# Each row gather waits for TensorE's side sum sixteen steps back instead of ten steps back

## The chip, the cores and the metric

The kernel runs on one core of one Trainium2 chip. The metric is the device time of one execution in microseconds (us), as the median of several runs. Engines are named as in the profile: PE is TensorE (PEld its weight loads), DVE is VectorE, ACT is ScalarE, POOL is GpSimd, SP is SyncE, whose queue starts the plain transfers.

## The reference

Four graph layers are applied one after the other to 12,500 nodes of 128 features and 200,000 edges sorted by target; each is added to its input and normalised. The parts that matter here are the edge parts: for each edge the row of its source node is fetched, a score is formed from it and the target's row, the scores are turned into weights by a softmax over the edges of one target, and the weighted rows are summed into the target. The first layer (two attention layers in it) reads:

```
xl = x @ Wl + bl
xr = x @ Wr + br
xj = xl[src]
e = jax.nn.leaky_relu(xj + xr[dst], NEG_SLOPE)
logits = e @ att
m = jax.ops.segment_max(logits, dst, num_segments=n)
ex = jnp.exp(logits - m[dst])
denom = jax.ops.segment_sum(ex, dst, num_segments=n)
alpha = ex / (denom[dst] + EPS)
out = jax.ops.segment_sum(alpha[:, None] * xj, dst, num_segments=n)
```

## The kernel before

Edges are laid out in tiles of 128, one tile being one **step**; 16 steps (`G`) make a **turn**, and a layer has 104 turns. Four edge stages share one set of functions, with an object `Edges` for each: E0 and E1 (gathering from `gather_a` and `gather_b`, one head), E2 (`gather_s`, scores from node scores alone, so that `vector` is false), and E3 (`gather_c`, eight heads). Between E1 and E2 lies another stage, S1, that scatters by source, and before, between and after them lie dense stages over the nodes.

In an edge stage every engine runs its own stream of instructions, and semaphores alone tie them together; nothing is reordered. In the turn with number `it`:

- SP (`sp_edges`, L658) loads the turn's tables into one of four slots: edge columns with the source indices (L665), one-hot rows, row values (L666, L667), step rows (L669; eight of them in E3). It waits until the sums of the turn four back have been added.
- POOL (`pool_edges`, L676) issues 16 gathers a turn (L687), one for each step: 128 rows of 512 bytes into `rows`, in slot `it % 4`. It waits for the tables of the turn (L682), for the block sums of the turn four back, which read the slot last (L684), and, before each gather, for a side sum (L686). This last wait is the subject. It guards no data: the slot is free by L684.
- PE (`side`, L708) goes through the turn in four chunks of four steps. For a chunk it waits until its four gathers have landed (L711), and then makes for each step a **side sum**: the target's row by a one-hot matrix (L721) plus the gathered row by the identity (L722). In E2 the side sum (L725) reads no gathered row. Behind each chunk's side sums PE makes one-hot distances for a later chunk (L705, L747), the **block sums** of the turn two back (L738), and a small transpose (L774, L779, L782 or L789, one for each chunk).
- ACT makes one-hot matrices (L811, L826) and the sloped scores (L862). DVE makes scores (L908, L915, L921), scans for the softmax, and adds block sums into the targets' sums (L951; L960 in E3).

A side sum of step `g` counts one up on the semaphore `side_sums`; `L.side.at(it, g)` is the count after step `g` of turn `it`, and `lag=1` takes the same step of the turn before. `hold_ge` is a wait. `Fori` loops run over four turns with the counts in registers; the first eight turns are written out.

Of the kernel before, what the change touches and what calls it, by code (L numbers as in the profile page):

```python
# [16 lines left out]
G = 16  # L17
# [1 line left out]
PEEL = 2 * U  # L19
CH = 4  # L20
NCH = G // CH
LEAD = 10
AW = 136
XW = 130
NSUM = 4
# [135 lines left out]
def turns(eng, n, depth, turn, ahead=0):  # L161


    assert ahead <= U
    end = n - U if ahead else n
    for i in range(PEEL):
        turn(Turn(i))
    with eng.Fori(PEEL // U, end // U) as j:
        for u in range(U):
            turn(Turn(u, j))  # L170
    for i in range(end, n + depth):
        turn(Turn(i))


def build(nc, a, out):
# [31 lines left out]
    with ExitStack() as ctx:  # L207
# [468 lines left out]
        def pool_edges(e, L):  # L676
            w = On(e, anchor)
            w.wait_ge(L.opened.at(0))

            def turn(it):  # L680
                u = it.slot()
                w.hold_ge(L.tab.at(it))  # L682
                for c in range(NCH):
                    w.hold_ge(L.block.at(it, c, lag=U))  # L684
                    for g in range(c * CH, (c + 1) * CH):
                        w.hold_ge(L.side.at(it, g - LEAD) if g >= LEAD else L.side.at(it, g + G - LEAD, lag=1))  # L686
                        e.indirect_dma_start(rows[:, u, g, 0:L.width], None, L.src_rows,  # L687
                                             bass.IndirectOffsetOnAxis(ap=edge_sb[:, u, g:g + 1].bitcast(I32), axis=0)
                                             ).then_inc(L.gat[c].sem(it), 16)
            turns(e, NG, 0, turn)  # L690
# [1786 lines left out]
```

## Time and profile before

| What | Value |
|---|---|
| median of 3 runs | 14976.3 us (14975.89 to 14977.52) |
| the profiled execution's own time | 14998.3 us |
| its span, first to last instruction | 14996.4 us |
| PE, DVE, ACT, POOL busy | 74%, 53%, 37%, 63% of the span |
| gathers in each edge stage | 1664 (104 turns of 16) |

Busy shares are averages over stages that are limited by different things, so they say little by themselves. "Idle before" in a row is how long the engine stood still just before an instruction, and the name behind the arrow is what the profile believes ended it: "issue" means that the profile sees no wait that ended there, and "remote" that a semaphore moved and the profile does not know by whom.

### The profile page before, as it was taken

To read this page: it belongs to the slowest core of one execution; us is meant where nothing else is said; L and a number is where in the kernel's file an instruction comes from. 1 tells how busy PE (TensorE), PEld (TensorE's weight loads), DVE (VectorE), ACT (ScalarE), POOL (GpSimd) and SP (SyncE) were. 2 spreads that over 40 slices of the span, in tenths; PEclk is the share of its full clock that TensorE was granted. 3 is DMA by queue.
4 is the path that set the end of the run, shared out by engine and by line. 5 is a ranking of instruction groups with operands and counts; after the bars stand their busy time and mean duration, and the time that the engine had idled before them with its cause. 6 is when DMAs were issued, how large, how long until landed. Compare 5 with 4: busy or idle time off the path is not lost.

```text
span 14996.4 us, 278163 instructions
## 1 busy us (share of the span) xinstructions
PE 11026.0 (74%) x60653; PEld 8678.6 (58%) x60653; DVE 7973.5 (53%) x29240; ACT 5541.4 (37%) x14105; POOL 9489.8 (63%) x8593
## 2 busy tenths in 40 slices
PE   5777777777777778888888875555555767777776
PEld 4666666666666666666666653344344556666664
DVE  6555555555555555555555553333333566666666
ACT  1444444344444444333333343333333622222223
POOL 3666666466666657888888865566666255655555
PEclk7887788788778775766666765555555877888777
DMA  3111111221111113444444452222222221222222
GB/s 87 45 45 44 44 45 45 88 80 44 45 44 45 44 40 44 39 39 39 39 39 39 39 104 58 44 45 45 45 45 45 60 52 48 50 49 49 50 50 56
DMA packets 808955, 748.01 MB, mean 50 GB/s; under 512 B 264685, under 2 KB 691174, under 8 KB 808254
## 3 DMA queue, kind: packets, MB, share of 16 engines
q0 software_dynamic: 453440, 550.05, 21.1%
q1 hardware_dynamic: 354814, 191.38, 4.9%
q14 instruction: 599, 4.91, 0.1%
q8 instruction: 102, 1.67, 0.0%
HBM read 548.62 MB, written 192.13 MB: 49 GB/s over the span
## 4 chain that ended last, share of the span: by engine, by line
PE 27%; another core or an unknown queue 15%; issue 13%; DMA 9%; DVE 7%; ACT 6%; POOL 2%; SPq 1%; DVEq 1%; ACTq 0%; POOLq 0%
DMA scatter_s<-dst_side 8%; PE bank L738 8%; PE bank L721 3%; PE bank L722 3%; PE bank L1214 3%; ACT oh_e L826 2%; PE bank L1220 2%; PE bank L1229 2%; PE bank L747 2%; PE bank L705 1%; POOL scatter_s L1181 1%; DVE agg L960 1%; DVE lrelu L915 1%; DVE agg L951 1%
## 5 line engine op out<-in xcount | busy, mean ns | idle before, releaser
L738 PE MATMUL bank<-rows,oh_e 128*128 128x130 f32 x9984 | 2172.6, 376 | 1578.7 <-ACT oh_e L826 1172.1
L1181 POOL DMA_INDIRECT scatter_s<-dst_side x1664 | 2568.6, 1544 | 551.9 <-DMA scatter_s<-dst_side 267.1
L738 PEld LDWEIGHTS bank<-rows,oh_e 128*128 128x128 f32 x9984 | 1804.0, 264 | 1918.7 <-issue 1036.4
L826 ACT ACTIVATE oh_e<-bank,weight,minus_w 128x128 f32<-128x128 f32 x4992 | 1880.3, 459 | 2378.4 <-remote 1620.8
L951 DVE SCALAR_TENSOR_TENSOR agg<-agg,rescale,bank 128x130 f32 x4992 | 1683.4, 337 | 1636.6 <-remote 792.6
L722 PE MATMUL bank<-rows,ident 128*128 128x128 f32 x9984 | 2335.9, 319 | 144.8 <-issue 141.1
L687 POOL DMA_INDIRECT rows<-gather_c,edge_sb x1664 | 1650.9, 992 | 1122.4 <-issue 443.9
L687 POOL DMA_INDIRECT rows<-gather_b,edge_sb x1664 | 1672.5, 1005 | 1061.9 <-issue 423.0
L687 POOL DMA_INDIRECT rows<-gather_a,edge_sb x1664 | 1669.1, 1003 | 1008.5 <-issue 412.0
L687 POOL DMA_INDIRECT rows<-gather_s,edge_sb x1664 | 1574.3, 946 | 1061.2 <-issue 443.2
L722 PEld LDWEIGHTS bank<-rows,ident 128*128 128x128 f32 x9984 | 1894.7, 235 | 159.7 <-issue 157.6
L862 ACT ACTIVATE lrelu<-bank 128x512 f32<-128x512 f32 x1248 | 751.2, 602 | 2734.9 <-PE bank L722 1900.8
L721 PE MATMUL bank<-dst_side,oh_t 128*128 x4992 | 1253.8, 338 | 202.5 <-issue 116.5
L721 PE MATMUL bank<-dst_side,hT 128*128 x4992 | 1232.0, 334 | 96.9 <-issue 93.2
L908 DVE TENSOR_TENSOR lrelu<-lrelu,bank 128x512 f32<-128x512 f32 x1248 | 850.5, 681 | 714.4 <-ACT lrelu L862 520.0
L705 PE MATMUL bank<-oh_rows,oh_w 5*128 5x512 bf16 x1664 | 788.6, 474 | 556.5 <-ACT oh_t L811 290.5
L721 PEld LDWEIGHTS bank<-dst_side,oh_t 128*128 128x128 f32 x4992 | 950.9, 236 | 311.4 <-issue 280.7
L721 PEld LDWEIGHTS bank<-dst_side,hT 128*128 128x128 f32 x4992 | 932.2, 232 | 194.5 <-issue 153.8
L1214 PE MATMUL bank<-rows,dst_side 128*128 128x130 f32 x3328 | 775.0, 399 | 343.1 <-DVE dst_side L1290 325.8
L1299 DVE SCALAR_TENSOR_TENSOR dst_side<-iota,edge_sb,bank 128x98 f32<-128x98 f32 x1664 | 432.4, 315 | 1115.9 <-PE bank L1220 1078.3
L738 PE MATMUL bank<-xw,oh_e 128*128 128x136 f32 x3328 | 620.4, 339 | 510.5 <-DVE xw L931 218.2
L1214 PEld LDWEIGHTS bank<-rows,dst_side 128*128 128x128 f32 x3328 | 653.2, 278 | 577.0 <-DVE dst_side L1290 359.6
(352 smaller groups left out, 18169.2 us busy)
## 6 DMA issues: line engine op xcount, KB each, us to landing
rows<-gather_a,edge_sb POOLq DMA_INDIRECT x1664
rows<-gather_b,edge_sb POOLq DMA_INDIRECT x1664
scatter_s<-dst_side POOLq DMA_INDIRECT x1664
rows<-gather_s,edge_sb POOLq DMA_INDIRECT x1664
rows<-gather_c,edge_sb POOLq DMA_INDIRECT x1664
rows<-scatter_s SPq DMA_DIRECT2D x56, 455.0 KB, 6.3
scatter_s<-zeros SPq DMA_DIRECT2D x64, 390.0 KB
edge_sb<-edge_tab SPq DMA_DIRECT2D x520, 40.0 KB
```

The lines of the kernel that those rows point to most:

```text
L687: e.indirect_dma_start(rows[:, u, g, 0:L.width], None, L.src_rows, bass.IndirectOffsetOnAxis(ap=edge_sb[:, u, g:g + 1].bitcast(I32), axis= ...
L705: e.matmul(bank[0][:, :], oh_w[:, :], oh_rows[:, it.slot(lag), c * CH * P:(c + 1) * CH * P], start=True, stop=True).then_inc(L.dist.sem, 1)
L721: e.matmul(o, oh, dst_flat[:, bass.ds(at[g], P)], start=True, stop=False)
L722: e.matmul(o, ident[:, :], rows[:, it.slot(), g, 0:P], start=False, stop=True).then_inc(L.side.sem, 1)
L738: ins = e.matmul(sum_bank(g)[:, (g % 2) * AW:(g % 2) * AW + L.aw], oh_e[:, g % 8, :], r, start=True, stop=True)
L826: e.activation(oh_e[:, g % 8, :], bank[7][:, (g % CH) * P:(g % CH + 1) * P], ACT.Relu, bias=weight[:, it.slot(2, 2), g:g + 1], scale=minus ...
L862: e.mul(lrelu[:, c % 2, :], bank[2 + c % 2][:, :], SLOPE).then_inc(L.sloped.sem, 1)
L908: e.tensor_tensor(lrelu[:, c % 2, :], lrelu[:, c % 2, :], bank[2 + c % 2][:, :], ALU.max).then_inc(L.larger.sem, 1)
L951: e.scalar_tensor_tensor(old, old, rescale[:, it.slot(2, 2), g:g + 1], sum_bank(g)[:, (g % 2) * AW:(g % 2) * AW + L.aw], ALU.mult, ALU.add ...
L1181: e.indirect_dma_start(scatter_s[k], bass.IndirectOffsetOnAxis(ap=S_.target[:, it.slot(1), g:g + 1], axis=0), S_.summed[:, g % 8, :], None ...
L1214: e.matmul(bank[6 + h % 2][:, (g % 2) * XW:(g % 2 + 1) * XW], S_.same[:, g % 8, :], rows[:, v, g, :], start=True, stop=True).then_inc(S_.b ...
L1299: e.scalar_tensor_tensor(S_.scratch[:, g % CH, 0:NB], iota[:, 0:NB], edge_sb[:, u, 4 * G + g:4 * G + g + 1], bank[5][:, (g % CH) * P:(g % ...
```

## The change

The constant `LEAD` goes, and with it the choice in L686. Before, the gather of step g waited for the side sum ten steps earlier: of the same turn where g is 10 or more, else of the turn before. Now it waits for the side sum of the same place in the turn before, sixteen steps earlier. Everything else stays, the waits for tables and block sums included. Line numbers below the removed constant fall by one.

```
-LEAD = 10
...
                 for c in range(NCH):
                     w.hold_ge(L.block.at(it, c, lag=U))
                     for g in range(c * CH, (c + 1) * CH):
-                        w.hold_ge(L.side.at(it, g - LEAD) if g >= LEAD else L.side.at(it, g + G - LEAD, lag=1))
+                        w.hold_ge(L.side.at(it, g, lag=1))
                         e.indirect_dma_start(rows[:, u, g, 0:L.width], None, L.src_rows,
```

No instruction of any engine changes its place. What differs on POOL is the count that a wait compares with, and that the first turn of a stage has no such wait at all. The start of E0 on POOL before, from the last index loads of the preparation (`tcoli`, L409) to the second turn:

```order
L409 DMA rows<-in_src_dram,tcoli 128x128 [waits edge_columns_made] x11
L687 DMA rows<-gather_a,edge_sb 128x128 [waits tables_in_slot0,rows_and_carry_set]
L687 DMA rows<-gather_a,edge_sb 128x128 x9
L687 DMA rows<-gather_a,edge_sb 128x128 [waits side_sums] x6
L687 DMA rows<-gather_a,edge_sb 128x128 [waits side_sums,tables_in_slot1]
```

And the same place now:

```order
L408 DMA rows<-in_src_dram,tcoli 128x128 [waits edge_columns_made] x11
L686 DMA rows<-gather_a,edge_sb 128x128 [waits tables_in_slot0,rows_and_carry_set]
L686 DMA rows<-gather_a,edge_sb 128x128 x15
L686 DMA rows<-gather_a,edge_sb 128x128 [waits side_sums,tables_in_slot1]
L686 DMA rows<-gather_a,edge_sb 128x128 [waits side_sums] x15
```

The six gathers of the first turn that waited for a side sum wait no more; from the second turn on each gather has its wait as before, on a lower count.

## Rows read from the trace of the kernel before

**Rows 1.** Busy time by stretch: E0, E1, then E2, E3.

```profile
core 0: us, PE busy (x) PEld busy (x) DVE busy (x) ACT busy (x) POOL busy (x), PEclk, DMA share, GB/s
220.00:2850.00 2630.00, 2031.69 (x12444) 1660.33 (x12444) 1433.82 (x4292) 1083.40 (x2760) 1668.83 (x1664) 0.81 0.18 45
2950.00:5585.00 2635.00, 2048.70 (x12444) 1668.62 (x12444) 1434.82 (x4295) 1087.42 (x2760) 1672.49 (x1664) 0.80 0.20 55
...
9090.00:11700.00 2610.00, 1408.97 (x7464) 1021.18 (x7464) 844.75 (x3365) 868.93 (x2345) 1574.27 (x1664) 0.50 0.21 46
12025.00:14780.00 2755.00, 2058.97 (x12627) 1700.82 (x12628) 1827.85 (x5108) 786.22 (x1949) 1650.52 (x1664) 0.81 0.20 50
```

**Rows 2.** What POOL's gathers waited for, E0's loop: releaser, us, times.

```profile
L687 POOL DMA_INDIRECT rows<-gather_a,edge_sb x1609: 941/947/1763, 301.4 to 2849.4; - x179
  PE bank L722: 311.6, 218
  remote: 201.7, 102
```

**Rows 3.** What PE waited for, E0's loop (us, times, longest).

```profile
PE bank L738 <- ACT oh_e L826: 237.1, 100, 5.7
PE bank L721 <- issue: 76.4, 102, 1.8
```

**Rows 4.** POOL in order of time, E0: start, us, gather, [idle before].

```profile
449.86 0.94 POOL L687 DMA_INDIRECT rows<-gather_a,edge_sb  x1 [1.86 <-PE bank L722]
451.11 1.67 POOL L687 DMA_INDIRECT rows<-gather_a,edge_sb  x1 [0.30 <-issue]
...
455.58 1.47 POOL L687 DMA_INDIRECT rows<-gather_a,edge_sb  x1 [0.30 <-issue]
```

**Rows 5.** PE's order of time: first and last late chunk of E0, E1, E3.

```profile
458.83 0.48 PE L721 MATMUL bank<-dst_side,hT 128*128 x2 [0.71 <-issue]
2847.47 0.48 PE L721 MATMUL bank<-dst_side,hT 128*128 x2 [1.08 <-issue]
3158.97 0.79 PE L721 MATMUL bank<-dst_side,oh_t 128*128 x2 [0.21 <-issue]
5582.06 0.48 PE L721 MATMUL bank<-dst_side,hT 128*128 x2 [0.90 <-issue]
12079.29 0.48 PE L721 MATMUL bank<-dst_side,oh_t 128*128 x2 [1.81 <-DMA rows<-gather_c,edge_sb]
14658.72 0.79 PE L721 MATMUL bank<-dst_side,oh_t 128*128 x2 [2.27 <-DMA rows<-gather_c,edge_sb]
```

**Rows 6.** SP's, POOL's and PE's order of time around one late chunk of E3.

```profile
13349.22 3.73 SPq L669 DMA_DIRECT2D step_sb<-step_tab  x8
13355.38 1.39 POOL L687 DMA_INDIRECT rows<-gather_c,edge_sb  x1 [3.05 <-issue]
13362.78 0.48 PE L721 MATMUL bank<-dst_side,oh_t 128*128 x2 [2.32 <-DMA rows<-gather_c,edge_sb]
```

**Rows 7.** PE and SP in order of time over two turns of E0.

```profile
1500.28 0.42 PE L774 MATMUL bank<-ident,masked 128*16 128x128 f32 x1
1520.33 0.29 PE L774 MATMUL bank<-ident,masked 128*16 128x128 f32 x1
1523.18 0.01 SPq L669 DMA_DIRECT2D step_sb<-step_tab  x1
1546.88 0.27 PE L774 MATMUL bank<-ident,masked 128*16 128x128 f32 x1
```

**Rows 8.** The chain that ended last, within E1: shares by line.

```profile
by line: another core or an unknown queue 21.0%; issue 15.4%; PE bank L738 15.1%; PE bank L721 12.6%; PE bank L722 11.9%; ACT oh_e L826 3.1%; PE bank L747 2.7%; PE bank L705 2.7%; DVE agg L951 2.7%; DVE lrelu L915 1.4%; DVE lrelu L908 1.2%;
```

**Rows 9.** DVE's longest wait in E2's loop, and who waited for gathers there.

```profile
DVE rescale L978 <- remote: 836.6, 81, 12.0
  DMA rows<-gather_s,edge_sb: 7.9, 1
```

**Rows 10.** DVE's groups in E0's loop: line, count, busy us, mean ns.

```profile
L915 DVE TENSOR_TENSOR lrelu<-lrelu,att 128x512 f32<-128x512 f32 x404 | 270.3, 669 | 0.8
```

More of the change, by code:

```diff
@@ L21 @@
 NCH = G // CH
-LEAD = 10
 AW = 136
@@ L685, in turn @@
                     for g in range(c * CH, (c + 1) * CH):
-                        w.hold_ge(L.side.at(it, g - LEAD) if g >= LEAD else L.side.at(it, g + G - LEAD, lag=1))
+                        w.hold_ge(L.side.at(it, g, lag=1))
                         e.indirect_dma_start(rows[:, u, g, 0:L.width], None, L.src_rows,
```

## The prediction

> **What bounds the kernel now.** I read the busy times by stretch first, since the change acts in the four edge stages alone. E0 and E1 take about 2630 us each, E2 2610 and E3 2755 [rows 1]: 104 turns of some 25.3 us (2630/104) in the first three and 26.5 us in E3. The reader is to see that no engine fills a turn. PE is busy 2032 of E0's 2630 us, at a granted clock of 0.81 of the full 2.4 GHz (the other level, 1.2 GHz, is 0.5, and E2 is there throughout). POOL's gathers fill 1669 us, 16 us a turn; with 0.30 us between two of them [rows 4] a gather costs 1.25 us, so 16 cost 20.0 us and POOL has some 5 us to spare in a mean turn, but none in a short one: the turn from 1500.28 to 1520.33 took 20.05 us, the next one 26.55 [rows 7].
>
> Next I asked what holds POOL. In E0's loop its gathers stood 311.6 us in 218 waits for the matmul that ends a side sum, and 201.7 us in 102 waits with an unknown releaser [rows 2]. The only waits in front of a gather inside a turn that can be that recent are those of L686, so POOL is held back by the ten-step rule about 500 us in E0, three to four times a turn for 1.6 us each (513/320).
>
> Then: does PE ever lack a gathered row? Most of PE's waits in E0 are for ACT's one-hot matrices (237.1 us in 100 waits before L738). Before L721 there are 76.4 us under "issue" [rows 3]. I went through the order of time and took those L721 that open a chunk and stand 1.7 to 2.6 us behind the end of their chunk's fourth gather. The first shows how [rows 4, 5]: the held gather waits 1.86 us, the fourth gather of the chunk ends at 455.58 + 1.47 = 457.05, and PE, which had been ready for 0.71 us, goes on at 458.83, 1.78 us later. That delay is the landing. In E0 there are 37 such chunks with 31.9 us of PE idle, in E1 42 with 35.8 us; every one of these 79 has a gather held by L686 among the last ten before it. E3 has 28 with 35.1 us; the first and the last of each stage are shown [rows 5]. So a late row costs PE 102.8 us in all, 0.7% of the run.
>
> **The change part by part.** It removes no instruction. It lowers the count that 16 waits a turn compare with, and takes six waits from the first turn of each stage; a wait that is met costs what lies between two gathers now, in both kernels.
>
> *E0 and E1.* A gather may run up to six steps, 7.5 us, further ahead. What holds it next is the table of its turn. In the turn of rows 7 the last table transfer is issued at 1523.18, 2.85 us behind L774 of 1520.33. From E3's row I take 2.4 us from last issue to first gather (13349.22 + 3.73 = 12.95 to 15.38 [rows 6]). So gathers of the next turn can start 5.3 us behind L774. The first four take 5.0 us and 1.8 us to land: 12.1 us behind L774. PE wants them at its next first chunk, about 15 us behind L774 even in a turn of 20 us (a chunk before that turn's end). So the table does not bind here, and the 67.7 us of late rows (31.9 + 35.8) should go. Bounds: nothing (another wait takes each place) to 67.7 us. PE works or issues for 60.4% of E1's chain (15.1 + 12.6 + 11.9 + 2.7 + 2.7 and 15.4 of issue) [rows 8]; the rest goes through waits of which many would have come anyway, ACT's above all. I take 0.55, a little under that share: 67.7 x 0.55 = 37 us.
>
> *E3.* Its late chunks are all the first of a turn. There the table comes last: eleven transfers, the last of them issued at 13352.95, first gather at 13355.38, and PE waits 2.32 us at 13362.78 [rows 6]. A later side-sum count changes nothing in that. I take 0; bounds 0 to 35.1 us.
>
> *E2.* Side sums there read no gathered row, and a gather was waited for once, 7.9 us, in the whole stage [rows 9]. I take 0. What sets E2 are waits like DVE's 836.6 us before L978, with unknown releaser; no gather stands in them.
>
> *The rest* (S1, dense stages) has no gather. Sum: 14998.3 - 37 = 14961 for the profiled execution. That one lies 22 us (0.15%) above the median of the runs, 14976.3, so I predict 14939.
>
> **The rivals.** A measurement of this kernel can tell about 0.2%, some 30 us, from no change.
>
> *B, hidden anyway.* PE's 79 late chunks last 0.86 us each on average (67.7/79), while its waits for ACT last 2.4 us (237.1/100 [rows 3]). If the next such wait simply grows by what the earlier one loses, the time is 14976. For it: the largest single share of E1's chain (21.0%) is an unknown releaser [rows 8], which no gather touches. Against it: PE and its issue still hold 60%.
>
> *C, slower: gathers that hold up DVE.* Gathers and DVE's products disturb one another already: a gather takes 947 ns as a rule and up to 1763 ns [rows 2], as the 1.67 us one [rows 4]. At present it is the gather that waits: L915, DVE's product of two operands in SBUF, has a mean of 669 ns over 404 [rows 10], with gathers running in most of the time. Gathers that start right behind the table instead of with PE's side sums come at other points of DVE's turn. If in each of the 312 turns of E0, E1 and E3 one gather now starts first and holds DVE for the difference, 0.82 us, that is 255 us of DVE; with a third of it on the path, 85 us, less the 37 gained: 14976 + 48 = 15024. It decides from about 135 such collisions on (37/0.82 x 3). Against it: not one of the long gathers shows such a thing today.
> The Trainium skill's page "SBUF — State Buffer", section "Who interferes with whom", says that a DVE instruction with two SBUF inputs excludes a GpSimd instruction that reads SBUF, and that whichever issues first makes the other wait in full. The trace agrees on the gather's side (1763 against 947 ns); on DVE's side no row here shows it, and by the rule the order of issue alone would decide, so it speaks against this change more than my rows do.
>
> *D, more than the waits.* A short turn of 20.05 us stands before a long one of 26.55 [rows 7], and 16 gathers cost POOL 20.0 us: a short turn leaves POOL no time to keep its lead, and the long one may be the price of that, in waits that the trace puts down to others. Long turns also let POOL catch up, so cause and effect are mixed. If the greater lead turns one turn in twenty of the 312 from long to short, 16 x 6.5 us = 104 us come on top: 14939 - 104 = 14835.
>
> **How the numbers follow.** Forecast 0.42 (its own range 14900 to 14966, from a full yield in E0 and E1 to a sixth of it), B 0.25, C 0.23, D 0.10. About 0.36 of the forecast's 0.42 lies below 14946, which is 0.2% under the median; with D that makes faster 0.46. B, the rest of the forecast and a weak C of 0.01 make the same 0.32; slower 0.22. The range reaches from D's time to C's, 14835 to 15024, which leaves about 2 in 10 outside on the far sides of these two.
>
> **What would show it.** Right: in E0 and E1 the held gathers inside a turn go, and POOL stands once a turn, before the first gather, for the table; the L721 that open a chunk lose their idle time; E0 and E1 are some 18 us shorter each, E2 and E3 as before. B: the same, but PE's waits for ACT's one-hot matrices grow by as much. C: L915 or L908 have a longer mean. D: more turns of about 20 us. Wrong altogether: the stages with no late rows, E2 above all, change by more than E0 and E1; then the phase of the gathers against the other engines matters in a way that no wait for them shows.

## The result and the profile after

The changed kernel takes 16396.7 us (median of 4 runs, 16373.0 to 16403.1), the kernel before 14976.1 us in the same comparison: a ratio of 1.0946 (95% interval 1.0932 to 1.0959). The prediction was 14939 us, with a range up to 15024; the change costs 1420 us instead. The profiled execution of after took 16391.6 us, its span is 16389.7 us.

Busy times by stretch: E0, E1, then S1, E2, E3 of the kernel after, with the same columns as [rows 1].

```profile
219.00:3114.00 2895.00, 2096.64 (x12378) 1705.42 (x12378) 1429.01 (x4279) 1092.00 (x2752) 1645.68 (x1664) 0.75 0.16 41
3222.00:6136.00 2914.00, 2089.03 (x12375) 1701.35 (x12376) 1426.69 (x4277) 1095.55 (x2752) 1645.46 (x1664) 0.75 0.18 49
6305.00:9390.00 3085.00, 2693.22 (x11572) 2010.98 (x11572) 1576.88 (x9089) 1093.22 (x2586) 2568.60 (x1664) 0.65 0.44 39
9646.00:12509.00 2863.00, 1401.74 (x7423) 1015.25 (x7423) 845.14 (x3353) 861.47 (x2335) 1574.46 (x1664) 0.50 0.19 42
12841.00:16165.00 3324.00, 2125.58 (x12588) 1730.26 (x12588) 1820.95 (x5092) 795.86 (x1942) 1610.20 (x1664) 0.73 0.17 41
```

The third row, S1, scatters and has no such gather; it takes as long as before. Against [rows 1] the four edge stages grow by 265, 279, 253 and 569 us, 1366 of the span's 1393. E2 grows like E0, though its side sums read no gathered row. No engine got more to do: E2's busy times differ by under 1%. In E0, E1 and E3 PE is busy some 40 to 67 us longer, at a granted clock of 0.73 to 0.75 in place of 0.80 to 0.81; in E2 the clock is at its lower level, 0.50, before and after, so there it is not the cause, and elsewhere PE's longer busy time is at most a quarter of the loss.

What POOL's gathers of E2 waited for (us, times), first in before, then in after. "issue" is mostly the 0.30 us that lies between any two gathers.

```profile
L687 POOL DMA_INDIRECT rows<-gather_s,edge_sb x1664: 941/947/1068, 9091.1 to 11698.1; - x185
  issue: 443.2, 1303
  remote: 373.8, 238
  PE bank L725: 216.1, 120
```

```profile
L686 POOL DMA_INDIRECT rows<-gather_s,edge_sb x1664: 941/947/1111, 9646.9 to 12508.5; - x185
  issue: 617.0, 1445
  PE bank L724: 353.6, 100
  remote: 298.5, 113
```

Before, POOL stood 358 times for 1.65 us each (589.9/358), 3.4 times a turn; now 213 times for 3.06 us (652.1/213), twice a turn. ("issue" hides some longer pauses: all pauses over 0.7 us are 355 before and 205 after.) So the gathers come in fewer and longer unbroken runs. And DVE and ACT wait longer in E2. Three "remote" rows, in before (beside L978's of [rows 9]) and in after (us, times, longest):

```profile
DVE agg L951 <- remote: 195.5, 34, 7.5
ACT oh_e L826 <- remote: 950.4, 124, 10.4
```

```profile
DVE agg L950 <- remote: 1042.0, 88, 14.0
DVE rescale L977 <- remote: 21.9, 1, 21.9
ACT oh_e L825 <- remote: 1224.6, 103, 14.0
```

DVE's long wait has moved from L978 (now L977) to L950. All "remote" rows of E2 together grow from 1176 to 1345 us for DVE and from 1257 to 1438 us for ACT, two thirds of what the two stand longer. In E0, E1 and E3 DVE's grow from 518 to 979, from 552 to 1011 and from 386 to 859 us. In both kernels every one of these waits ends with a count on a semaphore that PE alone counts up.

### The profile page after: what moved, and what is told of

Same layout as the page of the kernel before. It is cut to its first block, busy times and chain, and to the rows that moved or that the text cites. A ratio compares the mean times of both kernels' runs of the same rounds, so it can differ in the third digit from the quotient of the medians.

```text
span 16389.7 us, 278163 instructions
## 1 busy us (share of the span) xinstructions
PE 11291.8 (69%) x60653; PEld 8864.5 (54%) x60653; DVE 7973.3 (49%) x29240; ACT 5590.8 (34%) x14105; POOL 9401.4 (57%) x8593
## 4 chain that ended last, share of the span: by engine, by line
PE 33%; another core or an unknown queue 18%; issue 10%; DVE 7%; DMA 5%; ACT 4%; POOL 1%; DVEq 1%; ACTq 0%; SPq 0%; POOLq 0%
PE bank L737 9%; DMA scatter_s<-dst_side 5%; PE bank L720 4%; PE bank L721 4%; PE bank L1213 3%; PE bank L1219 2%; PE bank L1228 2%; PE bank L746 2%; PE bank L704 2%; ACT oh_e L825 2%; DVE agg L959 1%; DVE lrelu L914 1%; POOL scatter_s L1180 1%; PE bank L1222 1%
## 5 line engine op out<-in xcount | busy, mean ns | idle before, releaser
L950 DVE SCALAR_TENSOR_TENSOR agg<-agg,rescale,bank 128x130 f32 x4992 | 1682.8, 337 | 3414.8 <-remote 2880.1
L721 PE MATMUL bank<-rows,ident 128*128 128x128 f32 x9984 | 2412.2, 324 | 494.3 <-issue 488.6
L686 POOL DMA_INDIRECT rows<-gather_c,edge_sb x1664 | 1610.9, 968 | 1732.3 <-PE bank L721 835.9
L686 POOL DMA_INDIRECT rows<-gather_b,edge_sb x1664 | 1646.0, 989 | 1375.8 <-PE bank L721 510.7
L686 POOL DMA_INDIRECT rows<-gather_a,edge_sb x1664 | 1646.3, 989 | 1297.0 <-PE bank L721 524.1
L686 POOL DMA_INDIRECT rows<-gather_s,edge_sb x1664 | 1574.9, 946 | 1314.8 <-issue 617.0
L721 PEld LDWEIGHTS bank<-rows,ident 128*128 128x128 f32 x9984 | 1934.7, 237 | 535.9 <-issue 533.3
L720 PE MATMUL bank<-dst_side,oh_t 128*128 x4992 | 1360.9, 362 | 178.7 <-issue 154.7
L720 PE MATMUL bank<-dst_side,hT 128*128 x4992 | 1179.8, 315 | 319.2 <-issue 317.0
L704 PE MATMUL bank<-oh_rows,oh_w 5*128 5x512 bf16 x1664 | 823.7, 495 | 658.2 <-ACT oh_t L810 303.5
L720 PEld LDWEIGHTS bank<-dst_side,oh_t 128*128 128x128 f32 x4992 | 1040.7, 257 | 316.8 <-issue 287.3
L720 PEld LDWEIGHTS bank<-dst_side,hT 128*128 128x128 f32 x4992 | 864.7, 212 | 420.6 <-issue 360.8
L737 PEld LDWEIGHTS bank<-xw,oh_e 128*128 128x128 f32 x3328 | 533.5, 236 | 863.2 <-issue 462.1
```

Source lines behind the costliest of these rows:

```text
L704: e.matmul(bank[0][:, :], oh_w[:, :], oh_rows[:, it.slot(lag), c * CH * P:(c + 1) * CH * P], start=True, stop=True).then_inc(L.dist.sem, 1)
L720: e.matmul(o, oh, dst_flat[:, bass.ds(at[g], P)], start=True, stop=False)
L721: e.matmul(o, ident[:, :], rows[:, it.slot(), g, 0:P], start=False, stop=True).then_inc(L.side.sem, 1)
L737: ins = e.matmul(sum_bank(g)[:, (g % 2) * AW:(g % 2) * AW + L.aw], oh_e[:, g % 8, :], r, start=True, stop=True)
L950: e.scalar_tensor_tensor(old, old, rescale[:, it.slot(2, 2), g:g + 1], sum_bank(g)[:, (g % 2) * AW:(g % 2) * AW + L.aw], ALU.mult, ALU.add ...
```

## The experiments

Before these runs I held two theories. **R**: an unbroken run of gathers on POOL holds up the other engines, and the shorter lead helped because its waits broke the runs. **D**: the depth of the lead itself costs. Stage times in the table go from the first gather's start to the last one's end, in one profiled execution; "before" is the kernel before on the same chip. mix8, even10, even16m and even16n are medians of four to ten executions, the other runs one execution each.

| Run (lead or period) | E0 | E1 | E2 | E3 | Time, us | Before, us |
|---|---|---|---|---|---|---|
| before (profile) | 2630 | 2632 | 2608 | 2754 | 14998 | 14976 |
| after (profile) | 2895 | 2915 | 2863 | 3324 | 16392 | 14976 |
| lead8 | 2606 | 2611 | 2666 | 2706 | 14958 | 14939 |
| lead13 | 2636 | 2633 | 2679 | 2988 | 15328 | 14939 |
| leads (6, 7, 9, 6) | 2669 | 2654 | 2645 | 2738 | 15074 | 15005 |
| mix8 (8, 8, 10, 8) | 2645 | 2646 | 2604 | 2696 | 14985 | 15005 |
| burst12 | 3400 | 3407 | 3105 | 3581 | 17885 | 14939 |
| burst12n | 3434 | 3438 | 3158 | 3589 | 18043 | 15005 |
| burst12h | 3440 | 3450 | 3142 | 3665 | 18125 | 14981 |
| burst12p | 2867 | 2861 | 2665 | 2891 | 15655 | 14981 |
| paced | 2881 | 2859 | 2746 | 3054 | 15942 | 14939 |
| pause3 | 2805 | 2807 | 2744 | 3052 | 15791 | 14981 |
| flush1 | 2897 | 2908 | 2872 | 3333 | 16412 | 15005 |
| spread | 2909 | 2923 | 2821 | 3350 | 16413 | 14981 |
| even16 (1.42 us) | 2872 | 2873 | 2774 | 3031 | 15959 | 14903 |
| even16n (1.45 us) | 2835 | 2908 | 2828 | 3115 | 16077 | 14973 |
| even16m (1.49 us) | 2815 | 2813 | 2681 | 2953 | 15586 | 14973 |
| even16L (1.57 us) | 2706 | 2734 | 2618 | 2751 | 15171 | 14999 |
| even10 (1.42 us) | 2619 | 2621 | 2597 | 2719 | 14950 | 14903 |
| even10s (1.32 us) | 2619 | 2634 | 2678 | 2764 | 15063 | 14903 |

**The lead by itself.** lead8, and lead13 with 13 for 8:

```
-                        w.hold_ge(L.side.at(it, g, lag=1))
+                        w.hold_ge(L.side.at(it, g - 8) if g >= 8 else L.side.at(it, g + G - 8, lag=1))
```

> As before, but eight steps back in place of ten. Theory R (an unbroken run of gathers holds up the other engines; a wait that breaks it cures that): POOL is held as often as with ten or more, so the time is at or below before's, 14850 to 14980. Theory D (the depth of the lead itself costs, 1420 us for six steps, so some 237 a step): two steps less give up to 14500. Rows that come late speak against both: with eight steps, 10 us, in E0, E1 and E3 there would be more late rows, up to 15100, and E2 alone, which needs no row, would show the sign of R or D.

> Thirteen steps back. Theory D: half of the loss, about 15690, E2 half way between 2607 and 2862 us. Theory R: what counts is whether POOL is still held inside the turn; with thirteen the gathers 0 to 12 follow one another wherever the table came last, so most of the loss, above 16000, or none if POOL is still held at every chunk, below 15100.

Eight steps: E0, E1 and E3 are 21 to 48 us faster, E2 58 us slower. Thirteen: E0 and E1 do not move (2636 and 2633), E2 loses 71 of after's 255 us where D asked for half, E3 loses 234. So three more steps of depth cost nothing in two stages: there D falls, and their loss comes between 13 and 16.

leads and mix8 set the lead by stage:

```
+                self.lead = {id(gather_a): 8, id(gather_b): 8, id(gather_s2): 10, id(gather_c): 8}[id(src_rows)]
...
+                        w.hold_ge(L.side.at(it, g - L.lead) if g >= L.lead else L.side.at(it, g + G - L.lead, lag=1))
```

> The lead set by stage: 6 in E0, 7 in E1, 9 in E2, 6 in E3. Theory R: the smaller the lead the more often POOL stands and lets signals through, while late rows grow; E3, whose late rows came from tables, below lead8's 2706 us; E0 and E1 between 2560 (R alone) and 2750 us (rows late by three or four steps); E2 within 60 us of 2608. Theory D the same sign for E2 only: below 2608.

> Eight steps in E0, E1 and E3, ten in E2: the best of each stage in the runs so far. Stages are independent of one another in theory R, so the sum is before less 24, 21 and 48 us: 14845 against 14939, a ratio of 0.9938. If the stages' differences were one execution's chance, 14900 to 14990.

leads, with six and seven steps, takes 15074 us, above all 13 executions of before on that chip (14990 to 15022); which stage loses is not shown, since E0 and E1 of lead8 and mix8 differ by 39 and 35 us under the same rule. mix8 gives a ratio of 0.9987 (0.9978 to 0.9997), 20 us where the sum of the stages asked for 93: the stage differences of lead8 were largely those of one execution on one chip.

**Unbroken runs with a small lead.** burst12 keeps one wait a turn:

```
-                        w.hold_ge(L.side.at(it, g, lag=1))
+                        if g == 0:
+                            w.hold_ge(L.side.at(it, 12, lag=1))
```

> One wait a turn, before gather 0, for the side sum of step 12 of the turn before; the other fifteen gathers wait for no side sum. The lead is about four steps where the run starts and at most some eight where it ends, less than before's ten; the run of gathers is unbroken, 20 us. Theory R: as slow as after, 16000 or more, and E2 near 2860 us. Theory D: as before or faster, E2 at or below 2607 us; E0, E1 and E3 may lose by late rows, E2 not.

It takes 17885 us with a lead of some four steps where a run starts: D is out, R fits, and the trace shows how the time is lost. In E0, E1 and E3 the small lead also makes rows late: PE stands 502 us in E0 before chunks whose fourth gather had ended at most 2.6 us earlier (46 us in before). The stage to read is E2, whose side sums need no row; it takes 497 us more than before and 243 more than after. One run of gathers in E2, in order of time (start, us, engine, line; some rows left out):

```profile
12185.50 0.94 POOL L687 DMA_INDIRECT rows<-gather_s,edge_sb  x1 [10.50 <-PE bank L725]
...
12186.74 0.94 POOL L687 DMA_INDIRECT rows<-gather_s,edge_sb  x1 [0.30 <-issue]
...
12191.13 0.70 SPq L664 DMA_DIRECT2D edge_sb<-edge_tab  x1
...
12193.14 0.28 PE L792 MATMUL bank<-ident,decay_m 16*128 16x16 f32 x1
...
12193.27 0.58 PE L747 MATMUL bank<-oh_w,oh_rows 5*128 5x128 bf16 x4
...
12193.98 0.71 SPq L665 DMA_DIRECT2D oh_rows<-onehot_tab  x1
...
12197.51 0.70 SPq L666 DMA_DIRECT2D row_sb<-row_tab  x1
...
12201.01 0.01 SPq L668 DMA_DIRECT2D step_sb<-step_tab  x1
...
12204.22 0.94 POOL L687 DMA_INDIRECT rows<-gather_s,edge_sb  x1 [0.30 <-issue]
12205.97 0.17 DVE L978 TENSOR_SCALAR rescale<-bank 128x16 f32<-128x16 f32 x1 [15.07 <-remote]
...
12208.31 1.51 ACT L826 ACTIVATE oh_e<-bank,weight,minus_w 128x128 f32<-128x128 f32 x4 [16.01 <-remote]
...
12208.90 2.10 PE L738 MATMUL bank<-rows,oh_e 128*128 128x130 f32 x8 [14.43 <-ACT oh_e L826]
```

DVE's L978 waits for PE's transpose L792, which by its row ended at 12193.42; DVE starts 12.55 us later, 0.8 us behind the end of the run's last gather (12205.16). ACT's one-hot waits for L747, done at 12193.85, and starts 14.5 us later. The trace also keeps when a semaphore was counted: L792's count stands at 12205.95 and L747's at 12208.13, each just ahead of its waiter's start. PE then stands for ACT. SP's four table transfers, which take 1.5 us in a row elsewhere (even16L below), are issued over 9.9 us (median of this E2: 9.2; in E0 and E1 of the same run only 1.8 and 1.4). "remote" is no stranger here: it is PE's signal, so late that the profile no longer links it to the matmul. With POOL standing 10.5 us a turn the other engines do their work in that pause.

Going through the starts of E2's 96 middle turns of burst12, L978 starts over 3 us behind the end of L792 in all of them; in before in 78; in after in one, since DVE stands at L950 there. Signals that ACT or DVE give (ACT L826 to PE L738, 3088 cases; ACT L811 to PE L705, 386; DVE L1068 to ACT L848, 97) are never 1 us late. So it is what PE hands over that is held, and in E2 SP's issues. Whether the matmul itself ends late or only its signal, the profile can't tell, since it models the ends of matmuls.

**What in a gather does it.** burst12n fetches 64 bytes a row in place of 512 (516 in E2), burst12h 64 rows in place of 128; both leave out a part of the features:

```
-                        e.indirect_dma_start(rows[:, u, g, 0:L.width], None, L.src_rows,
+                        e.indirect_dma_start(rows[:, u, g, 0:16], None, bass.AP(L.src_rows.tensor, L.src_rows.offset, [(16, NB * P), (1, 16)]),
```

```
+                        e.indirect_dma_start(rows[0:64, u, g, 0:L.width], None, L.src_rows,
+                                             bass.IndirectOffsetOnAxis(ap=edge_sb[0:64, u, g:g + 1].bitcast(I32), axis=0)
```

> The burst12 kernel with each gather fetching 64 bytes a row from the front part of the table in place of 512 (516 in E2); as many rows, gathers and waits, so the features are not those of the reference and the output is not either. If it is the bytes that the gathers move which hold the signals, the time falls by 2000 us or more, to below 15900; if it is the gathers as such (their number, their rows, what POOL writes for them), it stays above 17500.

> The burst12 kernel with each gather fetching 64 rows in place of 128 (the other half of each tile's rows stays at one, so the features and the output are not the reference's). As many gathers and waits. If the rows of a gather are what has to be worked off before signals get through, half of them hold nothing up: below 16000 (part of which comes from shorter gathers on POOL, if they are shorter). If it is the gather as an instruction, above 17300.

Neither helps (18043 and 18125 us). An eighth of the bytes or half of the rows leaves the loss as it is; the amount of data isn't what holds PE.

**Pauses put back.** burst12p and pause3 add three memsets ahead of gather 8, to burst12 and to after; paced adds one ahead of each chunk:

```
+                    if c == 2:
+                        for k in range(3):
+                            w.hold_ge(L.paced.at(it, k - 1) if k else L.paced.at(it, 2, lag=1))
+                            e.memset(pace[:, :], 0).then_inc(L.paced.sem, 1)
```

> The burst12 kernel with three memsets of 1050 bytes (about 1 us each) on POOL ahead of gather 8, so that the run of sixteen falls into two of eight with some 3.5 us between. POOL gets 3 us a turn more to do and its gathers 8 to 15 come later; no wait changes. Theory R (signals of the other engines are held while a run of gathers is on and are let through in a pause of more than 1.5 us): E2 falls from 3105 us by 200 or more, E0 from 3400 by 200 or more, the whole below 17200. Theory P (only the place of the run against PE's turn counts): the same or slower, 17800 to 18200.

> The same three memsets in after's kernel. Theory R: there POOL already stands at two places (gathers 0 and 12), the third pause shortens the runs to eight at most: E2 from 2863 to 2700 or less, the whole 15600 to 16000, better than or like the paced run with the same sum of pauses in four pieces (15942). Theory D (depth of sixteen): 16400 or more.

> After's rule, and a memset of 800 bytes on one partition on POOL ahead of each four gathers, so that no run is longer than four though the lead stays sixteen. Theory R: most of the loss is gone, below 15400. Theory D: as after or slower, 16400 or more (POOL has 20 us of gathers and some 3 us of memsets in a turn of 28, so it does not bind).

burst12p is the clearest run of the study: 3 us a turn more work on POOL, and 2230 us less time (17885 to 15655, on another chip). The pause in E2, in order of time:

```profile
11029.79 0.94 POOL L696 DMA_INDIRECT rows<-gather_s,edge_sb  x1 [0.30 <-issue]
11030.73 0.96 POOL L692 MEMSET pace<- 1x1050 uint8 x1
11031.85 0.96 POOL L692 MEMSET pace<- 1x1050 uint8 x1 [0.15 <-POOL pace L692]
11032.96 0.96 POOL L692 MEMSET pace<- 1x1050 uint8 x1 [0.15 <-issue]
11033.11 0.17 DVE L1077 TENSOR_TENSOR shifted<-masked,bank 128x16 f32<-128x16 f32 x1 [14.49 <-remote]
11033.28 0.60 ACT L820 ACTIVATE oh_t<-bank 128x512 bf16<-128x512 f32 x1 [11.37 <-remote]
```

DVE and ACT had stood for 14.5 and 11.4 us and start 2.4 us into the pause, before the next gather, with POOL busy on memsets all the time: a busy POOL does no harm, gathers do. Late rows are not what the pauses cure: by the same count PE stands longer for them in E0 of burst12p, 855 us. pause3 gains 606 us on after, as R expected. paced has the same sum of pauses in four pieces and gains less, 454 us; both bounds of its expectation were missed. It would fit that a pause around one memset of 0.75 us is often over before PE's signal is through; that was not counted.

flush1 and spread did not do what they were built for:

```
+                    if c == 2:
+                        e.sem_inc(L.flush.sem, 1)
+                        w.hold_ge(L.flush.at(it))
```

```
+                        if g % 2 == 0:
+                            w.hold_ge(L.paced.at(it, g // 2, lag=1))
+                            e.memset(pace[:, g * 8:g * 8 + 16], 0).then_inc(L.paced.sem, 1)
```

> After's rule; ahead of gather 8 of each turn POOL counts a semaphore of its own up by one and waits until it sees the count. Theory R in its present form (while a run of gathers is on, signals of all engines are held and come some 2.8 us behind the run's end, as in the burst12 run; a pause of POOL lets them through): POOL's own signal is held too, POOL stands some 2 to 3 us at this place, and the kernel gets faster although POOL got more to do: E2 from 2863 to below 2720 us, the whole from 16397 to below 15800. Theory D (depth): no change or slower by the pause, 16400 to 16700. Theory S (the pause only has to exist, no matter what stands in flight): as the paced run, 15900.

> After's kernel with a memset of 16 bytes on POOL ahead of every second gather: no pause of a microsecond inside a run, but gathers come every 1.4 us or so in place of 1.25. Theory R with a backlog (each gather leaves more to be worked off than 1.25 us, so that signals get through only when it is empty): the backlog no longer builds, signals flow, E2 2700 us or less, the whole below 15900. Theory R with a need for real pauses: as after, 16300 to 16500.

In flush1 POOL saw its own count at once (the gap ahead of gather 8 in E2 stays near 0.3 us), so there was no pause and no change: POOL's own signals are not held, and R as I had worded it was too wide. In spread the memset of 0.10 us fits between two gathers and the period stays 1.25 us; it tested nothing.

**The period of the gathers.** A longer memset ahead of every gather stretches the period within a run. even16 and its relatives start from after (260, 310, 355 and 450 bytes), even10 and even10s from before (260 and 150):

```
+                        w.hold_ge(L.paced.at(it, g - 2) if g >= 2 else L.paced.at(it, g + G - 2, lag=1))
+                        e.memset(pace[:, g % 2 * 260:(g % 2 + 1) * 260], 0).then_inc(L.paced.sem, 1)
```

> After's rule with a memset of 260 bytes on POOL ahead of every gather, which should stretch the period of gathers in a run from 1.25 to about 1.45 us. Theory B (backlog: each gather leaves a fixed 1.4 us to be worked off, and signals pass when nothing is left): the backlog does not build, signals are 10 to 20 ns behind their instruction all the time, E2 at or below before's 2608 us and the whole below 15200. Theory N (pauses of 1.5 us are needed as such): no better than after, 16300 to 16700.

> The same memsets in before's kernel (ten steps back). Theory B: faster than before, since there too some signals are microseconds late; E2 2450 to 2600 us, E0 and E1 2500 to 2620, the whole 14400 to 14900, unless POOL, which then needs 23.2 us of a turn for its gathers, becomes the limit. Theory N: POOL's own waits shrink by what the memsets take, pauses get shorter and signals wait longer: 15100 to 15600.

> As even10 with memsets of 150 bytes, a period of about 1.35 us, just below 1.4. Theory B: the backlog grows by only 0.05 us a gather in place of 0.15, so between before and even10. Theory N: slower than before by some 0 to 300 us.

> As even16 with memsets of 450 bytes, a period of about 1.58 us, so that sixteen gathers take POOL 25.3 us, as much as a turn of before. Theory B (fixed 1.4 us a gather): with a period above it signals pass at once in the middle of runs, most within 0.1 us; E2, where POOL's own 104 x 25.3 = 2631 us are the floor, 2640 to 2720 us, although POOL has 2 us a turn more to do than in even16 (2774). Theory N: later than even16 by POOL's extra work, E2 2800 or more.

> As even16L with memsets of 355 bytes, a period of about 1.49 us. Theory B (fixed work of about 1.4 us a gather): signals still pass, E2 follows POOL down to 2484 to 2560 us, E0 and E1 2550 to 2650, E3 2650 to 2750, the whole 14500 to 14900, faster than before. If the bound lies above 1.49: signals late again, E2 2650 or more, the whole above 15300.

> The same with 310 bytes, about 1.46 us. Theory B with a bound of 1.4: E2 2423 to 2550 us, the whole at or below even16m's. With a bound between 1.46 and 1.49: slower than even16m by some 300 us or more.

The table names the period of each. At 1.42 and 1.45 us a part of the loss is gone, at 1.49 us more, and at 1.57 us nearly all: even16L takes 15171 us, with nine pauses over 0.7 us in the whole of E2. Its order of time there, in the middle of a long run of gathers:

```profile
11003.44 0.28 PE L798 MATMUL bank<-ident,decay_m 16*128 16x16 f32 x1
...
11004.09 0.17 DVE L984 TENSOR_SCALAR rescale<-bank 128x16 f32<-128x16 f32 x1 [1.10 <-PE bank L798]
11004.13 0.95 POOL L693 DMA_INDIRECT rows<-gather_s,edge_sb  x1 [0.16 <-POOL pace L691]
...
11016.30 0.36 SPq L666 DMA_DIRECT2D edge_sb<-edge_tab  x1
...
11016.78 0.95 POOL L693 DMA_INDIRECT rows<-gather_s,edge_sb  x1 [0.16 <-POOL pace L691]
11016.84 0.25 SPq L667 DMA_DIRECT2D oh_rows<-onehot_tab  x1
11017.28 0.51 SPq L668 DMA_DIRECT2D row_sb<-row_tab  x1
...
11017.83 0.32 SPq L670 DMA_DIRECT2D step_sb<-step_tab  x1
```

L798 and L984 are the L792 and L978 of burst12: DVE now follows 0.37 us behind PE's transpose (11003.72), between two gathers, and SP's tables go out within 1.5 us. In DVE's list of waits in E2 the "remote" rows make room for another, burst12 first, then even16L:

```profile
DVE rescale L978 <- remote: 1212.3, 82, 19.8
```

```profile
DVE logit L1101 <- DMA rows<-gather_s,edge_sb: 1127.8, 103, 19.7
...
DVE rescale L984 <- PE bank L798: 99.2, 89, 1.4
```

L984's longest wait under PE's name is 1.4 us (its start is over 3 us behind L798 in five of 96 turns), and the engines now wait for POOL: 1664 gathers of 1.573 us are E2's 2618 us. That also ends the hope for a faster kernel. I expected signals to pass from 1.4 us on, so that 1.49 us would give 14500 to 14900; even16m took 15586 (ratio 1.0405, 1.0388 to 1.0423), even16n 16077 (1.0729, 1.0709 to 1.0748): the bound lies between 1.49 and 1.57 us, where POOL itself needs a whole turn. DVE's "remote" rows of E2 sum to 1258 us at 1.49 and to 11 us at 1.57. even10 is a little slower than before (1.0027, 1.0012 to 1.0043) and even10s by about 1%: a period under the bound beside before's own pauses buys nothing. None of these beats before clearly; mix8 comes nearest.

## Why the prediction was wrong

**The step that failed** is the one on E2: "I take 0. What sets E2 are waits like DVE's 836.6 us before L978, with unknown releaser; no gather stands in them." Gathers did stand in them, though no wait names one. That wait [rows 9] is for PE's L792, which in 78 of 96 turns had ended over 3 us before, with gathers running in between; in burst12 the same row grows to 1212.3 us, in even16L it shrinks to 99.2 us (summed under PE's own name). In after the signal that comes late is mostly another, that for L950 (1042.0 us), and E2 loses 253 us. The same hidden term stood in E0, E1 and E3, where I counted only late rows. I took "waited for by nobody" for "felt by nobody".

**What the rule was for** follows from that. The prediction saw POOL held three to four times a turn [rows 2] and read it as time lost. These holds were the pauses in which PE's signals got through: POOL waits for PE, PE's signal comes late while gathers run, the run ends because of that wait, and the signals pass. Sixteen steps take four in ten of those pauses away in E2 and about one in seven in E0 (329 to 279), and what is left stands at fewer places, so that more gathers fall into long runs. Counted from the traces, a run ending at a pause over 0.7 us:

| Stage | Gathers in runs of eight or more, at 10, 13, 16 steps | Lost against before at 13, 16, us |
|---|---|---|
| E0 | 40%, 46%, 68% | 6, 265 |
| E2 | 56%, 71%, 78% | 71, 255 |
| E3 | 32%, 59%, 76% | 234, 570 |

**Late rows**: this mechanism was right. By the reading of [rows 5], one late chunk of 37 remains in E0, with no idle time of PE before it. Most late rows of E3 went too, which the prediction took at 0 (PE's idle time before the first side sum of a chunk falls from 54.8 to 15.7 us). Whether the 37 us of the sum were gained can't be read among 1366 us lost. (The forecast's own lower end is a slip: a full yield of 67.7 us gives 14909, not 14900.)

**The table's place**: that the table would hold POOL once a turn, ahead of gather 0, was right, but it is not the only pause left: a second one stands at gathers 8 to 12 in many turns. In after the first gather of a turn starts some 2.4 us behind the turn's last table issue, the delay of [rows 6], in all of the last 96 turns of E0 and of E2 and in 93 of E3; before, in none, none and 55. (The profile mostly names PE's side sum there.) At thirteen steps it does so in 40, 58 and 93 turns, in the order of what E0, E2 and E3 lose. So it fits that POOL, once the table sets its start, runs unbroken from there; even16L, where POOL is too slow to get that far, has no loss in E3 (2751 us). No run moved the table alone, and why E3, which I left at 0, loses twice as much as the others at sixteen steps stays open.

**Rival C** had the sign, not the mechanism. DVE's product in E0 after, line, count, shortest, median and longest ns:

```profile
L914 DVE TENSOR_TENSOR lrelu<-lrelu,att x412: 654/672/736, 232.5 to 3113.1; 128x512 f32<-128x512 f32 x138
```

Its longest is 736 ns, against a mean of 669 before [rows 10]: no gather holds it for 0.82 us. The rule of the Trainium skill's page "SBUF — State Buffer", section "Who interferes with whom", on two-input DVE instructions, is not what costs here: the trace shows no sign of it on DVE's side, and E2, which has none of these 512-column products, loses as much as E0. Rivals B and D are out with the sign.

**The last sentence** named the case: E2 changing as much as E0, by "the phase of the gathers against the other engines". It is not their phase but the length of their runs: burst12 and burst12p start their runs at the same step and differ by 2230 us. The chance for slower was 0.22, and no case priced it above 15024, since no price was taken from a wait with an unknown releaser.

## What to carry to other kernels

A wait that guards no data may still do work: it breaks an engine's stream, and something else may live on the breaks. Before loosening it, look at what the other engines do in its pauses, and whether they start there after waits with an unknown releaser. Where a wait's releaser is unknown, take the instruction that should have given the signal, compare its end with the waiter's start, and see which engine was active in between. And test a lead in two directions: same depth with other run lengths (burst12 against burst12p, after against pause3), and other depth with much the same runs (lead13 in E0 and E1).

## What was not expected of the hardware

While gathers followed one another every 1.25 us, what PE handed to DVE, ACT and POOL came up to 15 us late (L978 in burst12), and SP's four table issues took 9.9 us in burst12's E2; at 1.57 us it mostly came within 0.4 us (the median of L984 is 0.37) and SP took 1.5 us. The period alone does not decide about SP: in burst12's E0 and E1 its four issues took 1.8 and 1.4 us. In burst12's E2 ACT's signals to PE and DVE's to ACT were prompt, and in flush1 POOL's to itself. Neither the bytes (an eighth) nor the rows (half) of a gather changed that. A pause around a memset of 0.75 us helped in part; in one of 3.4 us what stood went on.

Why stays open. It would fit that each gather leaves a fixed piece of work, of about 1.5 us by the even runs, to something that PE's signals and SP's issues also pass through; no run shows that thing. The Trainium skill's page "NOTIFIC — the notification-queue block", section "Overflow: three behaviours, one of which stalls the engine", says that the block which writes the profiler's records holds back inside rather than lose a record there, in both of its modes. Whether recording takes part here, no run tells apart.
